# Gate scores read from a PSUM bank, and scatter sums added four groups at a time, in a graph network layer

## What is computed

```python
h = maximum(layernorm(x), 0)
att = sigmoid(h[src] @ W_att[:128] + h[dst] @ W_att[128:] + b_att)
messages = (h[src] @ W_msg + b_msg) * att
aggregated = segment_sum(messages, dst, num_segments=num_nodes)
gi = aggregated @ W_ih.T + b_ih
gh = h @ W_hh.T + b_hh
r, z = sigmoid(i_r + h_r), sigmoid(i_z + h_z)
n = tanh(i_n + r * h_n)
h_new = (1 - z) * n + z * h
out = x + gamma * (h_new - mean) * rsqrt(var + eps) + beta
```

## Time and profile before

| what | value |
|---|---|
| median of 3 runs | 2257.26 us (2253.13 to 2259.02) |
| profiled execution, first to last instruction | 2256.1 us |
| PE busy | 2055.7 us (91%) |
| DVE busy | 2012.9 us (89%) |
| ACT busy | 1996.3 us (88%) |
| POOL busy | 1660.4 us (74%) |
| mean granted TensorE clock | 0.965 |

### The profile page before, as it was taken

The page is one execution under the profiler, slowest core; times in us unless marked ns, Lnnn a source line. Parts: engine busy times, 40 slices in busy tenths (PEclk is TensorE's granted clock), DMA queues, the critical chain, the costliest instruction groups (busy, mean ns, idle before and its releaser), DMA issues.

```text
span 2256.1 us, 53903 instructions
## 1 busy us (share of the span) xinstructions
PE 2055.7 (91%) x18202; PEld 1994.3 (88%) x18202; DVE 2012.9 (89%) x4413; ACT 1996.3 (88%) x6980; POOL 1660.4 (74%) x1578
## 2 busy tenths in 40 slices
PE   3536999999999999999999999999999999999997
PEld 3525999999999999999999999999999999999996
DVE  5967899999999999999999999999999999999974
ACT  1368999999999999999999999999999999999943
POOL 4575777777777777777777777777777777777760
PEclk8865999999999999999999999999999999999998
DMA  6862222222222222222222222222222222222236
GB/s 164 237 172 62 56 60 62 59 60 60 62 62 62 63 58 64 61 63 59 63 59 62 59 61 60 63 60 62 60 61 63 59 62 60 61 61 64 58 108 231
DMA packets 167473, 171.57 MB, mean 76 GB/s; under 512 B 79462, under 2 KB 131736, under 8 KB 166944
## 3 DMA queue, kind: packets, MB, share of 16 engines
q0 software_dynamic: 49856, 102.96, 20.3%
q1 hardware_dynamic: 114564, 61.63, 10.5%
q10 hardware_dynamic: 2776, 3.52, 0.7%
HBM read 141.32 MB, written 26.65 MB: 74 GB/s over the span
## 4 chain that ended last, share of the span: by engine, by line
ACT 53%; PE 23%; DVE 14%; issue 7%; DMA 2%; SPq 1%; POOL 0%; ACTq 0%; DVEq 0%
ACT big L901 41%; PE ps L1456 12%; ACT gate_ring L897 9%; DVE big L1200 4%; PE ps L1441 4%; PE ps L1451 3%; DVE gate_ring L1184 2%; DVE key_hot L1170 1%; PE ps L1462 1%; PE ps L1463 1%; DVE lo_hot L1163 1%; DMA big<-in_x_dram 1%; DVE big L1129 1%; DMA row_ring<-node_table,set_idx 1%; ACT n_blk L906 1%
## 5 line engine op out<-in xcount | busy, mean ns | idle before, releaser
L773 POOL DMA_INDIRECT row_ring<-node_table,set_idx x1480 | 1571.8, 1062 | 473.4 <-issue 334.5
L901 ACT ACTIVATE big<-set_score,big 128x128 f32<-128x128 f32 x5096 | 1633.2, 394 | 81.0 <-PE ps L1456 80.7
L1456 PE MATMUL ps<-big 128*128 128x128 f32 x10192 | 1447.4, 281 | 0.0
L1456 PEld LDWEIGHTS ps<-big 128*128 128x128 f32 x10192 | 1265.0, 193 | 0.0
L1200 DVE TENSOR_TENSOR big<-ps,big 128x784 f32<-128x784 f32 x832 | 802.0, 964 | 10.2 <-ACT big L901 5.4
L1441 PE MATMUL ps<-gate_ring,row_ring 128*128 128x64 f32 x2960 | 534.8, 263 | 78.0 <-DVE gate_ring L1184 72.7
L1441 PEld LDWEIGHTS ps<-gate_ring,row_ring 128*128 128x128 f32 x2960 | 454.0, 194 | 124.4 <-DVE gate_ring L1184 110.7
L1184 DVE SCALAR_TENSOR_TENSOR gate_ring<-lane,set_rel,gate_ring 128x64 f32<-128x64 f32 x1480 | 412.9, 279 | 140.1 <-ACT gate_ring L897 135.0
L897 ACT ACTIVATE gate_ring<-set_win,row_ring 128x64 f32<-128x64 f32 x1480 | 493.2, 341 | 30.5 <-DMA row_ring<-node_table,set_idx 27.3
L1451 PE MATMUL ps<-key_hot,lo_hot 128*128 128x196 bf16 x3328 | 425.8, 250 | 14.4 <-DVE key_hot L1170 9.5
L1170 DVE TENSOR_TENSOR key_hot<-lane_key,set_key 128x1568 bf16<-128x1568 bf16 x416 | 402.0, 966 | 0.0
(11 more groups left out here) (129 smaller groups left out, 917.2 us busy)
## 6 DMA issues: line engine op xcount, KB each, us to landing
row_ring<-node_table,set_idx POOLq DMA_INDIRECT x1480
big<-in_x_dram SPq DMA_DIRECT2D x48, 256.0 KB, 5.6
h_blk<-hT_spill SPq DMA_DIRECT2D x97, 64.0 KB
node_table<-big SPq DMA_DIRECT2D x24, 258.0 KB
hT_spill<-big SPq DMA_DIRECT2D x24, 256.0 KB, 4.8
out_dram<-big SPq DMA_DIRECT2D x24, 256.0 KB
set_win<-dst_scores SPq DMA_DIRECT2D x148, 32.0 KB
set_score<-dst_scores SPq DMA_DIRECT2D x52, 64.0 KB
```

Source lines behind the costliest of these rows:

```text
L773: nc.gpsimd.indirect_dma_start(row_ring[:, t % ROWS_RING, :], None, table, bass.IndirectOffsetOnAxis(ap=set_idx[:, t // SET % 2, t % SET:t ...
L901: return nc.scalar.activation(a_buf[b % 2][:, h, :], set_score[:, b % 2, :], ACT.Sigmoid, bias=m_all[:, h, D:ROW])
L1456: return nc.tensor.matmul(ps[:, AM_BANK, 0:P], m_all[:, h, 0:D], a_buf[b % 2][:, h, :], start=h == 0, stop=h == HI - 1)
```

## The change

Score tiles are copied into PSUM once, by ACT, and all gates read them there: `keep_score(b)` copies the 128 scores of a dense block, `keep_window(g)` the 64 scores of a group. They use bank 6, two slots of 128 and four of 64 columns. That bank is made free because all four windows of sums of a set now lie in bank 5. DVE adds the four windows of a set together, before the mask of the second tile of the next set (`add_set`). PE doesn't scatter in the first two tile steps of a set, and scatters two tiles each in the third and the fourth (`scattered_at`). The list of GRU jobs is made with groups counted by sets. SP waits for the kept score instead of the finished gates before it loads the next score.

```diff
-GROUP_LAG = 3
+SET_LAG = 2
 def groups_before(u, s):
-    return GROUPS if u == BLOCKS and s > LAST_TILES + GROUP_LAG else max(0, tiles_before(u, s) - GROUP_LAG - 1) // GROUP
+    if u == BLOCKS and s > LAST_TILES + SET_LAG:
+        return GROUPS
+    return GROUPS_S * (max(0, tiles_before(u, s) - SET_LAG) // SET)
+def scattered_at(t):
+    k, i = t // SET, t % SET
+    if k == 0 or i > 3:
+        return (t,)
+    return ((), (), (t - 2, t - 1), (t - 1, t))[i]
...
+        def ps_window(g):
+            return ps[:, SP_BANK, (g % GROUPS_S) * WIN:(g % GROUPS_S + 1) * WIN]
+        def ps_score(b):
+            return ps[:, SCORE_BANK, (b % 2) * P:(b % 2 + 1) * P]
+        def ps_dst_scores(g):
+            return ps[:, SCORE_BANK, 2 * P + (g % GROUPS_S) * WIN:2 * P + (g % GROUPS_S + 1) * WIN]
...
-                    sp.wait_ge(gates_dense, u + 1)
+                    sp.wait_ge(scores_kept, u + 1)
                     load_score(u + 2)
...
+            def keep_score(b):
+                act.wait_ge(score_loaded[b % 2], 16 * (b // 2 + 1))
+                nc.scalar.copy(ps_score(b), set_score[:, b % 2, :]).then_inc(scores_kept, 1)
+            def keep_window(g):
+                if g % GROUPS_S == 0:
+                    set_ready(act, g // GROUPS_S)
+                nc.scalar.copy(ps_dst_scores(g), set_win[:, g // GROUPS_S % 2, g % GROUPS_S, :]).then_inc(windows_kept, 1)
             def gate(t):
                 wait_reuse(act, tiles_summed, t + 1 - GATES_RING)
-                if t % SET == 0:
-                    set_ready(act, t // SET)
+                if t % GROUP == 0:
+                    act.wait_ge(windows_kept, t // GROUP + 1)
                 act.wait_ge(gathered[t % ROWS_RING], 16 * (t // ROWS_RING + 1))
-                nc.scalar.activation(gate_ring[:, t % GATES_RING, :], set_win[:, t // SET % 2, t % SET // GROUP, :], ACT.Sigmoid,
+                nc.scalar.activation(gate_ring[:, t % GATES_RING, :], ps_dst_scores(t // GROUP), ACT.Sigmoid,
                                      bias=row_ring[:, t % ROWS_RING, D:ROW]).then_inc(gates_ready, 1)
+                if t % GROUP == 4 and t // GROUP + 1 < GROUPS:
+                    keep_window(t // GROUP + 1)
             def dense_gate(b, h):
-                return nc.scalar.activation(a_buf[b % 2][:, h, :], set_score[:, b % 2, :], ACT.Sigmoid, bias=m_all[:, h, D:ROW])
+                return nc.scalar.activation(a_buf[b % 2][:, h, :], ps_score(b), ACT.Sigmoid, bias=m_all[:, h, D:ROW])
...
             def add_group(g, base):
-                dve.wait_ge(tiles_summed, g * GROUP + GROUP)
+                if g % GROUPS_S == 0:
+                    dve.wait_ge(tiles_summed, (g // GROUPS_S + 1) * SET)
...
+                        if t % SET == SET_LAG - 1 and t > SET:
+                            add_set(t // SET - 1)
                         mask(t)
-                        if t % GROUP == GROUP_LAG and t > GROUP:
-                            add_group(t // GROUP - 1, bases[t // GROUP - 1])
...
-                if t % GROUP == 0:
-                    wait_reuse(pe, groups_added, g - 1)
-                nc.tensor.matmul(ps[:, SP_BANK + g % 2, 0:WIN], row_ring[:, t % ROWS_RING, 0:D],
+                if t % SET == 0:
+                    wait_reuse(pe, groups_added, g)
+                nc.tensor.matmul(ps_window(g), row_ring[:, t % ROWS_RING, 0:D],
...
-                    if t is not None:
-                        scatter(t)
+                    for of in scattered_at(t) if t is not None else ():
+                        scatter(of)
```

28 lines of the change are left out of this document (18 added, 10 removed).

## The result

| | kernel before | changed kernel |
|---|---|---|
| median of the runs | 2257.89 us (2253.13 to 2259.02, 4 runs) | 2268.61 us (2265.77 to 2274.98, 4 runs) |
| ratio | 1 | 1.0059 [1.0044, 1.0073] |
| span of the profiled execution | 2256.1 us | 2264.1 us |

The changed kernel is slower by 0.6%, where 0.5% faster had been forecast. The experiments ran on two kinds of chip, told apart by the time of the kernel before. On the first kind, to which the table belongs, the kernel before takes about 2258 us; on the second kind it takes about 2569 us.

The account below looks back on a forecast made before the run. It took POOL's gathers, 1.368 us each without a pause, to bound the kernel. Sum: 2256.1 - 11 + 0 + 0 + 1.3 = 2246.4, plus 1.2 for the median, given as 2247 us, 0.5% less; range of 8 in 10: 2195 to 2288.

Parts of the forecast that it names:

- What bounds the kernel now: Steady stretch, 330 to 2130 us: POOL runs without a pause at 1.368 us per gather and is the limit.
- The stretch from 2163 to 2185 us: Last building unit, ACT without dense gates: 16 gathers still take 1.365 us each, used as decisive evidence for POOL.
- the hits: Gathers beginning inside a bf16 DVE instruction stand until it ends, by a two-port lock: 0.12 us lost per gather.
- POOL's rate after the change: Steady stretch: gathers still fill it at 1.36 to 1.375 us each, ACT waiting hundreds of us for rows.
- The start: Before 330 us: earlier gates eat POOL's ring waits, moving the end of its work up 7 to 13 us; 11 taken.
- The steady stretch: Main loop: POOL keeps 1.368 us per gather, so 0 us, with bounds of -35 and +33 us.
- Rival 2: Main loop: hits become more frequent at fixed places of a beat, 1.392 us per gather, 2280 us; chance 0.24.
- The additions: DVE, four window adds together: 0.9 us once in 40 tiles, covered by 125 us free; 0 us, at most 33.
- The held scatters: PE holds two scatters up to two tile steps; POOL's slot comes 2.7 us late, hidden by the ring: 0 us.
- The third job in the last unit: End of the program: the list counted by sets puts three GRU jobs rather than two there, +1.3 us on PE.
- The gates and the copies: ACT: gates from PSUM 0.25 us start to start instead of 0.292; 200 copies at 0.20 us; net relief about 236 us.

Follow-up runs that it names:

- b_skip: Kernel before without the gather of every tenth tile after the first ten (147 of 1480), first kind of chip: 2256.5 us, 0.9995 of the kernel before.
- a_split2: Changed kernel with each `key_hots` cut into two halves at different steps, first kind of chip: 2251.96 us, 0.9970 of the kernel before.
- b_banks2: Changed kernel's set-wise adds and job list, gates reading SBUF, no copies, sums in two banks, no held scatters, first kind of chip: 2275.82 us, 1.0071.
- b_hold3: Kernel before with only the held scatters of the change, first kind of chip: 2261.78 us, 1.0009 of the kernel before.
- a_even2: Changed kernel with the extra place taking a gather job only when three are ready, not two, first kind of chip: 2273.49 us, 1.0070.
- a_split: Changed kernel with each `key_hots` cut into two halves at different steps, second kind of chip: 1.0109 of the kernel before.

## Why the prediction failed, point by point

**What bounds the kernel now: wrong, and the error is in one inference.** I took POOL's lack of pauses for proof that POOL sets the pace. b_skip refutes it: without a tenth of the gathers the time stays, 0.9995 [0.9985, 1.0005]. No pause says only that the others are not slower; it doesn't say that they are faster. I had the other half of the evidence in hand: ACT hardly waited for rows, 3.4 us in 1800. If POOL had been the pace, ACT would have waited. An engine without pauses whose customer doesn't wait for it either runs level with something, and by the trace the something was ACT's loop. The stretch from 2163 to 2185 us showed truly what an idle ACT does, and it is what the changed kernel does; it was no evidence on the kernel before.

On the cause of the hits, the rule that I took from the Trainium skill is one for VectorE's two-port modes, and the hots are `tensor_tensor`, which by the same page have none (see a_split2). That a gather waits for them is the traces' own finding and stays.

**POOL's rate after the change: right.** I forecast 1.36 to 1.375 us per gather with hundreds of us of waits for rows, and got 1.373 us and, less than I said, 129.2 us of waits. As both limits lay level, the wrong inference cost nothing here: a faster ACT could gain nothing in the steady stretch. That is luck, not insight.

**The start, -11 us: mis-sized; -2.0 us measured.** I meant the 11.3 us of POOL's ring waits from 182 to 330 us to vanish and to leave the gathers as short as they were. POOL's group there after the change:

```profile
L794 POOL DMA_INDIRECT row_ring<-node_table,set_idx x103 | 112.1, 1089 | 37.6 <-issue 20.1 <-PE ps L1484 17.5
```

The gaps shrank by 42.7 - 37.6 = 5.1 us, so that 37.6 - 103 x 0.305 = 6.2 us of ring waits are left of the 11.3, and the gathers grew by 112.1 - 106.9 = 5.2 us. So the forecast failed here in two ways: about half of the waits stayed, and what the other half gave back went into longer gathers. This is the largest part of the miss, 9 us.

**The steady stretch, 0 us: mis-sized by +7.5 us.** The bounds of -35 and +33 held it. Rival 2 named the mechanism and the side, at 1.392 us per gather and 2280 us; the step was a fifth of that. The count of hits, from one trace of each kernel, fits it: 31.1% of the gathers start inside one of the hots after the change and 29.9% before, at the same mean of 1.308 us, and 0.012 x (1.308 - 0.960) = 0.004 us per gather is most of the step of 0.005. Why they are more frequent, and whether it comes from fixed places of a beat, isn't shown.

**The additions, 0 us: wrong in its price and in its cover.** I multiplied 0.216 us, the recorded length, for both orders. From start to start one alone is 0.14 us and one in a row 0.36. The bound of 33 us was near what DVE lost, 25 to 29 us. The 125 us that DVE had free on average did not cover it: with gates from SBUF, adds and list together cost 16.6 us (b_banks2); in the changed kernel POOL's pace covers a part that I can't give, as the adds apart weren't run with it on the first kind of chip.

**The held scatters, 0 us: right** on the first kind, where b_hold3 tests it on the kernel before and POOL has no wait over 0.3 us in the steady stretch of the changed one, and wrong on the second, where POOL already waits for slots.

**The third job in the last unit, +1.3 us:** the time behind the last gather grew by 2.5 us, on the side forecast and twice the size. That the job is the reason isn't tested; a_even2 keeps it there.

**The gates and the copies: right.** Six dense gates in a row on ACT's timeline after the change:

```profile
1004.08 1.65 ACT L935 ACTIVATE big<-ps,big 128x128 f32<-128x128 f32 x6
```

(1.65 - 0.40) / 5 = 0.25 us from start to start, 0.292 before; gates of tiles went from 0.238 to 0.196 us, and the copies take 0.14 (64 columns) and 0.20 us (128), where 0.20 was taken. The Trainium skill ("Perfetto Trace Analysis", section "Optimizing Scalar/DVE Operations") has the same 42 ns between the two memories, and the trace agrees.

The sum of what was measured is -2.0 + 7.5 + 2.5 = +8.0 us, where the forecast had -11 + 0 + 1.3. The larger part of the miss is a gain that was expected and didn't come. The range of 8 in 10, 2195 to 2288 us, held the result; what was wrong is the side.

## What to carry to other kernels

An engine without a pause is the pace only if somebody waits for it; look at both ends of its queue, and if neither waits, two loops run level and relieving one gains nothing. Before counting on what a change frees, price what it needs to make room for itself: here that half alone cost 19 us, and with the freed engine the whole still cost 11. An instruction's price in a row of dependent ones isn't its recorded length, and a delay that a ring hides on one chip can be paid on another where the ring has less slack.

## What the runs showed of the hardware that I had not expected

- The recorded length of a dense gate rose from 394 ns to 449 ns when its source went from SBUF to PSUM, while the distance between starts fell from 0.292 to 0.249 us. ACT's busy time in the steady stretch therefore fell by 144 us only, to 1582, where the distances had led me to 1510. Here the recorded lengths of overlapping instructions don't measure work.
- A 128x64 add costs 0.14 us of DVE behind an independent instruction and 0.36 us behind an add that it waits for by a semaphore.
- Relief of other engines changes the gathers: their mean was 1.038 us while POOL waited for the ring, 1.089 us in the same stretch with half of that wait, 1.054 with DVE relieved, 1.107 with one gather in ten left out, and 1.049 with split hots.
- Chips differ by 14% for the same program, with nearly the same length of single instructions on ACT, and they rank variants of a kernel differently: a_split is 0.3% faster than the kernel before on the one kind and 1.1% slower on the other.
